# Early-fusion block on one core: the pair norm's moments on ScalarE, patches ahead of transposes, three weight splits inside the first expert tiles

## What is computed

```python
h = concat([patch_embed(x, W, b)[hilbert order], txt], axis=1)   # 32 images, 333 tokens, D = 192
h = h + attn(layernorm(h))      # depthwise conv over 9 taps, softmax over 9 taps, window sum; 12 heads
h = h + moe(layernorm(h))       # 8 experts, top 2, capacity 1.2*N/8, silu gate, hidden 512
# layernorm: m = mean(x); v = var(x); (x - m) / sqrt(v + 1e-5)
```

## Time and profile before

| | |
|---|---|
| median of 3 runs | 1454.35 us (1453.72 to 1455.99) |
| the profiled execution | 1453.47 us |
| its span in the trace | 1451.7 us |
| PE, DVE, POOL, ACT busy | 83%, 70%, 48%, 32% of the span |
| first expert matmul | 839.0 us after the start |

### The profile page before, as it was taken

The page is one execution under the profiler, slowest core; times in us unless marked ns, Lnnn a source line. Parts: engine busy times, 40 slices in busy tenths (PEclk is TensorE's granted clock), DMA queues, the critical chain, the costliest instruction groups (busy, mean ns, idle before and its releaser), DMA issues. The chain is left out here.

```text
span 1451.7 us, 30799 instructions
## 1 busy us (share of the span) xinstructions
PE 1202.5 (83%) x8700; PEld 1012.9 (70%) x8701; DVE 1019.9 (70%) x2367; ACT 464.8 (32%) x1197; POOL 691.9 (48%) x530
## 2 busy tenths in 40 slices
PE   6987998997989898951642089999999999999995
PEld 6766777775767777640422078988898898898895
DVE  4117959999999999999586366666666666666663
ACT  1111222333222232311113344444444444444442
POOL 1000221656656666754647724554545454545454
PEclk9999999898989998975675589999999999999998
DMA  9995554565646363548611446544444444444442
GB/s 306 402 318 138 141 166 106 161 177 163 169 114 208 104 180 85 160 100 219 191 46 48 124 61 64 68 56 62 61 63 57 63 58 63 57 63 59 61 60 28
DMA packets 215171, 175.31 MB, mean 121 GB/s; under 512 B 121864, under 2 KB 198694, under 8 KB 215104
## 3 DMA queue, kind: packets, MB, share of 16 engines
q1 hardware_dynamic: 170128, 115.36, 32.5%
q0 software_dynamic: 34720, 34.38, 14.5%
q10 hardware_dynamic: 10256, 24.73, 4.6%
HBM read 69.24 MB, written 88.47 MB: 109 GB/s over the span
## 5 line engine op out<-in xcount | busy, mean ns | idle before, releaser
L1238 POOL DMA_INDIRECT out<-yb,meta x182 | 298.0, 1638 | 313.4 <-DMA out<-yb,meta 204.0
L129 POOL DMA_INDIRECT expert_inputs<-slot_rows,slots x176 | 237.9, 1351 | 85.6 <-issue 60.2
L1023 PE MATMUL bankK<-normedT,conv_w 128*128 128x333 f32 x864 | 274.0, 465 | 0.0
L1308 DVE TENSOR_TENSOR hidden<-silu,bankU 128x256 f32<-128x256 f32 x364 | 153.3, 421 | 141.7 <-PE bankU L1346 94.3
L1264 ACT ACTIVATE silu<-bankG 128x256 f32<-128x256 f32 x364 | 139.8, 384 | 304.6 <-PE bankG L1346 304.6
L1023 PEld LDWEIGHTS bankK<-normedT,conv_w 128*128 128x128 f32 x864 | 167.1, 199 | 76.2 <-issue 9.4
L1359 PE MATMUL bankY<-expert_weights,hidden_high 128*128 x728 | 179.2, 246 | 0.8
L1360 PE MATMUL bankY<-expert_weights,hidden_high 128*128 x728 | 179.3, 246 | 0.0
L1361 PE MATMUL bankY<-expert_weights,hidden_low 128*128 x728 | 179.1, 246 | 0.0
L713 DVE TENSOR_TENSOR prod<-window_values,kb 128x960 f32<-128x960 f32 (+1 forms) x135 | 167.9, 1253 | 3.6
L731 DVE TENSOR_TENSOR hidden_group<-hidden_group,prod 128x960 f32<-128x960 f32 (+1 forms) x135 | 169.1, 1252 | 0.5
(11 more groups left out here) (162 smaller groups left out, 2295.2 us busy)
## 6 DMA issues: line engine op xcount, KB each, us to landing
patches<-in_x SPq DMA_DIRECT2D x16, 1536.0 KB, 8.5
expert_inputs<-prod ACTq DMA_DIRECT2D x6, 3430.0 KB, 23.3
token_rows<-rowbuf SPq DMA_DIRECT2D x32, 492.0 KB
window_values<-token_rows SPq DMA_DIRECT2D x32, 264.0 KB, 5.4
hidden_group<-token_rows SPq DMA_DIRECT2D x32, 264.0 KB, 7.1
window_values<-token_rows SPq DMA_DIRECT2D x32, 192.0 KB, 5.7
kb<-token_rows SPq DMA_DIRECT2D x32, 148.5 KB, 4.6
token_rows<-rowbuf SPq DMA_DIRECT2D x32, 148.0 KB
```

The lines of the kernel that those rows point to most:

```text
L129: nc.gpsimd.indirect_dma_start(out=xslots[:, :], out_offset=bass.IndirectOffsetOnAxis(ap=idx[g % 2][:, k, r:r + 1], axis=0), in_=xrow[g % ...
L1023: mm = T_.matmul(bankK[(u + t) % 2][:, 0:L], conv_w[:, t // 2, k, :], qT[u][:, t, k:k + L], start=(k == 0), stop=(k == K - 1))
L1238: nc.gpsimd.indirect_dma_start(out=out[:, :], out_offset=bass.IndirectOffsetOnAxis(ap=meta[t % NMETA][:, c, 0:1], axis=0), in_=yb[v][:, c, ...
L1308: V.tensor_tensor(hf[j % 2][:, :], sg[j % 2][:, :], bankU[j][:, 0:TS], ALU.mult)\
```

## The change

1. Mean and variance of a pair leave DVE. ACT makes them in a new step `moments(p)`: six Identity passes over the 192 columns that add up to the scaled negative mean, a wait, then six Square passes with that mean as bias that add up to the variance. `moments(p+1)` stands at the top of the iteration; `moments(p+2)` is set two instructions at a time behind the six copies of `routing_out`. POOL's `pair_norm` reads the new tiles.
2. PE runs `patch(p+2)` ahead of `transposes(p+1)`, and `patch(p+3)` ahead of `transposes(p+2)`.
3. Splits: experts 0 and 1 at the end of block one, 2 to 4 at the start of block two, and 5, 6, 7 within tiles 1, 3 and 5 of the first body. The loads of experts 6 and 7 go behind the loads of tiles 0 and 1 on SP. Each tile of the first body waits for as many splits as it can need.

```diff
-EARLY = 4
+EARLY, MIDDLE = 2, 5
...
+                def moments(p):
+                    u = p % 2
+                    act.wait_ge(h_in_rows, 2 * p + 2)
+                    act.wait_ge(txt_loaded[u], 16 * (p // 2 + 1))
+                    wait(act, ln_step, NLN * p)
+                    wait(act, tq_ready, 3 * p - 3)
+                    settled(act)
+                    def spare(n):
+                        return qn[u][:, n // 2, n % 2 * D:(n % 2 + 1) * D]
+                    for n in range(6):
+                        ins = nc.scalar.activation(spare(n), rowb[u][:, n // 2, n % 2, D:2 * D], ACT.Identity,
+                                                   scale=-1 / (D * ROOT), accum_out=mean[:, n:n + 1])
+                        if n == 5:
+                            ins.then_inc(mean_done, 1)
+                        yield
+                    act.wait_ge(mean_done, p + 1)
+                    for n in range(6):
+                        ins = nc.scalar.activation(spare(n), rowb[u][:, n // 2, n % 2, D:2 * D], ACT.Square,
+                                                   bias=mean[:, n:n + 1], scale=1 / ROOT, accum_out=var[:, n:n + 1])
+                        if n == 5:
+                            ins.then_inc(var_done, 1)
+                        yield
...
@@ routing_out
                         nc.scalar.copy(xTr[n % 2][:, :], bankT[n % 2][:, 0:384]).then_inc(tr_evac, 1)
+                        if beside:
+                            next(beside)
+                            next(beside)
...
@@ ACT's order
+                all_of(moments(0))
                 normalise(0)
                 tiles_out(0)
                 for it in range(NG):
                     p = 2 * it
+                    all_of(moments(p + 1))
                     normalise(p + 1)
...
+                    following = () if last(p + 1) else moments(p + 2)
                     if it > 1:
-                        routing_out(it - 2, 0, NQ)
+                        routing_out(it - 2, 0, NQ, following)
+                    else:
+                        all_of(following)
...
@@ DVE, norm(p) becomes patches_out(p)
-                    dve.wait_ge(txt_loaded[u], 16 * (p // 2 + 1))
-                    dve.wait_ge(h_in_rows, 2 * p + 2)
-                    for c in (2, 0, 1):
-                        for m in range(2):
-                            ins = V.bn_stats(stats[:, 2 * c + m, :], rowb[u][:, c, m, D:2 * D])
-                    ins.then_inc(stats_done, 1)
-                    dve.wait_ge(stats_done, p + 1)
-                    wait(dve, ln_step, NLN * p)
-                    settled(dve)
-                    for n in range(6):
-                        ins = V.bn_aggr(mv[:, n, :], stats[:, n, :])
-                    ins.then_inc(aggr_done, 1)
...
@@ POOL
                 def pair_norm(p):
-                    pool.wait_ge(aggr_done, p + 1)
+                    pool.wait_ge(var_done, p + 1)
                     wait(pool, qn_ready, p)
-                    layer_norm(mv[:, :, 0], mv[:, :, 1], tmp6, rs, 6, ln_step, NLN * p)
+                    layer_norm(mean[:, :], var[:, :], tmp6, rs, 6, ln_step, NLN * p, back=3)
...
@@ PE's order
-                    transposes(p + 1)
                     if p + 2 < NPAIR:
                         patch(p + 2)
+                    transposes(p + 1)
...
+                    if p + 3 < NPAIR:
+                        patch(p + 3)
                     if not last(p + 1):
                         transposes(p + 2)
-                    if p + 3 < NPAIR:
-                        patch(p + 3)
...
@@ block two
+            SPLIT_AT = {1: MIDDLE, 3: E - 2, 5: E - 1}
...
-                for e in (E - 2, E - 1):
-                    load_w(sp, e, raw_of(e), w_loaded[2])
...
+                        if first_body(i) and t < 2:
+                            load_w(sp, E - 2 + t, raw_of(E - 2 + t), w_loaded[2 + t])
...
-                for e in range(EARLY, E):
-                    if e == E - 2:
-                        act.wait_ge(w_loaded[2], 128)
+                for e in range(EARLY, MIDDLE):
                     split_high(act, e, raw_of(e))
...
+                        if first_body(i) and t in SPLIT_AT:
+                            e = SPLIT_AT[t]
+                            if e >= E - 2:
+                                act.wait_ge(w_loaded[e - E + 4], 64)
+                            split_high(act, e, raw_of(e))
...
                         if t or not first_body(i):
                             evac_y(i, t - 1)
+                        if first_body(i) and t + 1 in SPLIT_AT:
+                            split_low(dve, SPLIT_AT[t + 1], raw_of(SPLIT_AT[t + 1]))
...
-                    if first_body(i) and t == 0:
-                        pe.wait_ge(w_low, E)
+                    if first_body(i):
+                        pe.wait_ge(w_low, max(MIDDLE, t + 1))
```

More of the change, by code:

```diff
@@ L31 @@
 EPS = 1e-5
+ROOT = D ** 0.5
 NPAIR = B // 2
@@ L90, in build @@
         tile_experts = sb("tile_experts", [128, NBODY], i32)
-        w_loaded = [sem(f"w_loaded{n}") for n in range(3)]
+        w_loaded = [sem(f"w_loaded{n}") for n in range(4)]
         w_high, w_low, last_sent = sem("w_high"), sem("w_low"), sem("last_sent")
@@ L157, in build @@
             ca = [in_slab(f"conv_attn{u}", [128, 3, L]) for u in range(2)]
-            stats = sb("stats", [128, 6, 6])
-            mv = sb("mean_var", [128, 6, 2])
+            mean = sb("scaled_minus_mean", [128, 6])
+            var = sb("variance", [128, 6])
             rs = sb("rstd", [128, 2, 6])
             tmp6 = sb("tmp6", [128, 2, 6])
-            cst = sb("pool_constants", [128, 3, R])
+            cst = sb("pool_constants", [128, 4, R])
             vx = [sb(f"window_values{b}", [128, (R + 2 * PAD) * D]) for b in range(2)]
@@ L225, in build @@
             h_in_rows = sem("h_in_rows")
-            stats_done = sem("stats_done")
-            aggr_done = sem("aggr_done")
+            mean_done = sem("mean_done")
+            var_done = sem("var_done")
             ln_step, ln2_step = sem("ln_step"), sem("ln2_step")
@@ L391, in _ @@
             def _(pool):
-                for k, c in enumerate((-0.5, EPS, -1.0)):
+                for k, c in enumerate((-0.5, EPS, -1.0, ROOT)):
                     nc.gpsimd.memset(cst[:, k, :], c).then_inc(cst_set, 1)
-                pool.wait_ge(cst_set, 3)
+                pool.wait_ge(cst_set, 4)
                 pool.wait_ge(zeroed, 1)
@@ L400, in _, with layer_norm @@
                                    channel_multiplier=FILL_ROWS).then_inc(empty_set, 1)
-                def layer_norm(mean, var, tmp, res, n, done, at):
+                def layer_norm(mean, var, tmp, res, n, done, at, back=2):
                     TTn = nc.gpsimd.tensor_tensor
@@ L410, in layer_norm @@
                     pool.wait_ge(done, at + 3)
-                    TTn(res[:, 1, :], tmp[:, 1, :], cst[:, 2, 0:n], ALU.mult).then_inc(done, 1)
+                    TTn(res[:, 1, :], tmp[:, 1, :], cst[:, back, 0:n], ALU.mult).then_inc(done, 1)
                 def pair_norm(p):
-                    pool.wait_ge(aggr_done, p + 1)
+                    pool.wait_ge(var_done, p + 1)
                     wait(pool, qn_ready, p)
-                    layer_norm(mv[:, :, 0], mv[:, :, 1], tmp6, rs, 6, ln_step, NLN * p)
+                    layer_norm(mean[:, :], var[:, :], tmp6, rs, 6, ln_step, NLN * p, back=3)
                 def slice_norm(g, s):
@@ L498, in fill, with all_of @@
                            .then_inc(fill_done, 16)
+                def moments(p):
[20 more added lines that the diff above has]
+                        yield
+                def all_of(steps):
+                    for _ in steps:
+                        pass
                 def normalise(p):
@@ L549, in high_parts, with routing_out @@
                     nc.scalar.copy(xrow16[g % 2][:, ss, 0:D], xn[:, ss, :]).then_inc(xh_ready, 1)
-                def routing_out(g, lo, hi):
+                def routing_out(g, lo, hi, beside=()):
                     for n in range(lo, hi):
@@ L637, in _, with patches_out @@
                 V.memset(zeros, 0.0).then_inc(zeroed, 1)
-                def norm(p):
+                def patches_out(p):
                     u = p % 2
@@ L895, in _ @@
                 dve.wait_ge(first_loaded, 16 * NFIRST)
-                norm(0)
+                patches_out(0)
                 dve.wait_ge(const_loaded, NCONST)
@@ L922, in part @@
                         n -= 1
-                norm(1)
+                patches_out(1)
                 for it in range(NG):
@@ L928, in _ @@
                     if it:
-                        norm(p + 1)
+                        patches_out(p + 1)
                     if it > 1:
@@ L944, in _ @@
                     if not last(p + 1):
-                        norm(p + 2)
+                        patches_out(p + 2)
                     part(6)
```

## The result

The changed kernel takes 1469.53 us (median of 4 runs, 1469.08 to 1469.84), the kernel before 1454.03 beside it: a ratio of 1.0103, 95% interval 1.009 to 1.0116. It is slower by 1.0%. The profiled execution's span is 1468.0 us against 1451.7. By the page DVE is busy 992.4 us (1019.9 before) and ACT 540.8 (464.8).

A forecast was written before the change was run, and what follows sets the result against it. A closed loop through POOL, ACT and PE (80.1 us) was to replace DVE as the bound in iterations 4 to 6. Block one -2 and tail +5.2 made +3.2 on 1453.47: 1456.7, forecast 1457 us, range 1439 to 1471.

The forecast's parts named there:

- second rival: Moments on ACT are dear, 8.0 us a pair, deciding from 6.5 us on: +15, 1469 us, slower; chance 0.17.
- The moments on ACT: Twelve passes over 192 columns a pair plus a wait: 6.0 us, between 3.6 and 8.0.
- at 83 or more rival 2: Sign set on iterations 4 to 6: 80 to 81 us as forecast, 77 rival 1, 83 or more dear moments.
- The counts' wait: PE's 1.95 us wait in iteration 6 for routing counts from DVE, forecast to shrink below 0.5 us.
- The loop: Closed through POOL, ACT and PE from iteration 4 on: 80.1 us once around, against PE's floor of 77.2.
- their landing: POOL's wait for the fifteen scatters to land; the forecast's loop sum had no term for it.
- PE's stretch: Loop term on PE from its transposes to the router's first copy, less the patch: 13.4 us.
- The clock: PE's granted clock falls behind a stall at transposes(p+1) in iterations 4 to 6: 0.5 us an iteration.
- The early iterations: Iteration 2 gains 2 us, iteration 3 gains 3; start and iterations 0 and 1 together 0, between -5 and +5.
- the bare chain of pair 0: At the start nothing covers pair 0's moments: 6.0 us for 2.3, +3.7.
- The tail: After block one: -1.5 at the first matmul, +3 tile 1's late rows, +3.7 splits of experts 6 and 7: +5.2.
- which of the banks: PE's two gate banks hold 2.2 us of matmuls ahead of ACT; four up banks cover DVE's 3.1 us.

The follow-up runs named there:

- two separate cuts: Changed kernel with moments(p+1) issued ahead of normalise_slice(it-1, 0): 0.9926 of before; changed kernel with 9 of 15 late scatters ahead of pair_norm(p+2): 0.9900.
- The filler: Changed kernel with 24 patch matmuls made twice in iterations 4 to 6, ahead of transposes(p+1) where PE stalls: 1.014 of the kernel before.
- scatters_in_three_parts: Changed kernel with 9 of POOL's 15 late scatters issued between slice_norm(it-2, 1) and pair_norm(p+2), 6 left behind it: 0.9900 of the kernel before.

## Why the prediction was right in its range and wrong in its forecast

The forecast was 1457, measured were 1469.5: inside the range, on the slower side that had 0.41, and 12.5 us from the forecast. That it lies inside says little: the range was 32 us wide and held a loss as well as a gain, and of the 16 us that the span grew by the forecast had 3. 1469 was the second rival's figure, but its cause is not the one that acted, so that match is luck.

- **The moments on ACT.** 6.0 us forecast, 4.95 measured, within the bounds of 3.6 and 8.0. The second rival is wrong in its cause: the sum does get out by an instruction of its own, but hidden. The passes come every 0.35 and 0.44 us with the sums' instructions between them. The sign that I set for it ("at 83 or more rival 2") would have misled, since any longer loop gives it. The Trainium skill, ScalarE: Activation LUTs, section What ACT_TABLE_LOAD costs, prices a pass at 186 ns and 0.833 ns per column, with 93 ns more for a pointer operand. For 192 columns that is an estimate of 346 ns, or 439 with one pointer, and the trace agrees with 352 and 445. It doesn't show the 93 ns saved back to back here, and so the estimate of 3.6 us made from that page was too low.
- **DVE.** Busy -27.5 us, forecast -35; ACT +76.0 for +96. The counts' wait of the earlier trace rows is gone, as said.
- **The loop.** Its place was right, shown by two separate cuts, and its parts by the rows of the trace after. The step that failed is its sum, 80.1 for 85.2. Term by term, from slice to slice: slice and cast 3.8 (3.9 forecast), moments 5.0 (6.0), `pair_norm` twice 5.4 (4.8), `normalise` 3.6 (3.6), PE to the first copy 17.6 (13.4), copies and last passes 14.3 (14.5), scatters 21.7 (21.8), their landing 2.7 (left out), `low_parts` 3.5 (2.6), `slice_norm` 2.2 (4.7). Two terms make the miss of 5.1: the landing, 2.7, a wait that I had named in POOL's program and put at nothing, and PE's stretch, 4.2 too short as I took it from a kernel without the stall. The others sum to -1.8 (mostly moments -1.0 and `slice_norm` -2.5, against `pair_norm` +1.2 and `low_parts` +0.9).
- **The clock.** I put 0.5 us an iteration on PE's half clock and forgot that PE's stretch is itself a term of the loop: a stall slows transposes, scores and a conv, that lengthens the loop, and that lengthens the stall. The filler shows 3.3 of the 4.2 us as the clock's. That they come back as time of the iteration follows from the terms of the loop; no run shows it by itself.
- **Iterations 4 to 6** then follow: +1.3, +5.4, +3.9 where I had 0. The loop grows into its length; the stalls at `transposes(p+1)` are 4.3, 4.6 and 6.5 us for my 2 to 4. **Iteration 7**: +8.2 for +3, its stall 14.2 for "over 8".
- **The early iterations.** Iteration 2 gained 5.6 where I had 2, and where the rest comes from I didn't locate; iteration 3 gained 3.2 for 3. Start and iterations 0 and 1 lost 5.2, just past the end of my -5 to +5; of it 3.8 is the bare chain of pair 0, priced at 3.7. That iteration 0 gains nothing from the new PE order was the moments' doing: without them it is 5 us shorter.
- **The tail.** The way to the first matmul gained 1.9 (-1.5 forecast, one slow scatter fewer). The first matmul is 24.6 us behind POOL's first scatter of block two, near my 22 to 24. Tile 1 was late by 1.5 us, not 3, and the splits of experts 6 and 7 cost PE hardly anything, not 1.85 us each: one row of 0.18 us is all that PE waited for silu. These two make 1.7 of the 3.1 us that the tiles lost; the rest I didn't locate. I had let PE wait until ACT's split and the silu behind it were over; the trace shows that they were covered, not which of the banks did it. Tail +1.2 for +5.2, at the low end of +1 to +8. Alone, the splits make no difference.
- **Scatters.** The Trainium skill, SBUF — State Buffer, section Who interferes with whom, infers that a tensor_tensor leaves descriptor generation alone. The traces speak against it for these scatters (1.89 to 1.96 us beside 960-wide steps, below). Keeping the trace's durations was right: 21.7 us for the fifteen against 21.8.

Against the forecast, iterations 4 to 7 are 15.7 us longer, start and iterations 0 to 3 1.4 longer, and the tail is 4.0 shorter: 13.1 us, of which the tail's error hid a part of the loop's.

## What to carry to other kernels

Where engines run in fixed order, walk every loop that a moved step closes, with each wait in it counted and with the bound engine's own stretch at the clock that it will have behind a stall. Room on an engine (ACT busy 37%) says nothing about a step that stands between two waits: on top of the new PE order the same 5 us of moments cost 1.8% in one order of ACT and POOL, and nothing that can be told (0.0% and -0.3%) in two others. Where an engine waits and the profile names no cause, look at when the other engines got its results: here PE's rows ran up to 7 us ahead of its semaphores, and a wait of 7.22 us that seemed to be DVE's was mostly PE's. Before moving work, look for what else may be moved out of its way; nine scatters put into POOL's idle 19 us were worth 2.0%.

## What the runs showed of the hardware

How long a scatter takes goes with what DVE does beside it. In scatters_in_three_parts five in a row beside 960-wide multiply and add steps take 1.89 to 1.96 us and come every 2.2 to 2.26, as two such steps do (1.16 and 1.15 us, one pair every 2.26); beside 1152-wide steps of 1.35 us most take 0.97 to 1.1. Why the narrower steps hold a scatter up more isn't shown:

```profile
517.88 1.96 POOL L130 DMA_INDIRECT expert_inputs<-slot_rows,slots  x1 [0.30 <-issue]
520.14 1.95 POOL L130 DMA_INDIRECT expert_inputs<-slot_rows,slots  x1 [0.30 <-issue]
522.40 1.96 POOL L130 DMA_INDIRECT expert_inputs<-slot_rows,slots  x1 [0.31 <-issue]
...
537.51 1.08 POOL L130 DMA_INDIRECT expert_inputs<-slot_rows,slots  x1 [0.30 <-issue]
538.89 0.97 POOL L130 DMA_INDIRECT expert_inputs<-slot_rows,slots  x1 [0.30 <-issue]
```

PE's clock falls behind a stall: after the 6.45 us in iteration 6 of the changed kernel the granted clock was 0.50 over the next 7 us, nine transposes took 2.22 us instead of 1.25 and a conv 7.82 us instead of 5.25.
